# TensorE's order inside a step of the second attention: value and key products ahead of the output products

## What is computed

```python
q = (x @ w_q)...; k = (x @ w_k)...; v = (x @ w_v)...      # 32 query heads, 8 key/value heads of 128
lq = x @ w_lq; lk = (lq @ w_lk)...; lv = (x @ w_lv)...    # 32 latent key/value heads
q, k, lk = rope(q), rope(k), rope(lk)
attn = causal_attn(q, repeat(k, 4), repeat(v, 4), scale)
lat  = causal_attn(q, lk, lv, scale)
out = attn @ w_o + lat @ w_lo
```

## Time and profile before

| what | value |
|---|---|
| median of 3 runs | 2500.93 us (2497.93 to 2501.97) |
| the profiled execution | 2504.47 us, of it the span 2502.3 us |
| busy share of the span | PE 91%, PEld 80%, DVE 71%, ACT 58%, POOL 63% |
| mean granted TensorE clock | 0.955 of full |
| HBM over the span | 36 GB/s |

### The profile page before, as it was taken

How to read it: one execution, slowest core, us unless ns; L and a number is a source line. 1 busy time by engine, 2 the same in 40 slices (tenths; PEclk the granted TensorE clock), 3 DMA queues, 4 the chain that set the end, 5 groups by cost and what they waited for, 6 DMA issues and landing times. The chain is left out here.

```text
span 2502.3 us, 44127 instructions
## 1 busy us (share of the span) xinstructions
PE 2282.1 (91%) x14117; PEld 2003.4 (80%) x14117; DVE 1771.3 (71%) x3132; ACT 1452.4 (58%) x3980; POOL 1576.2 (63%) x1336
## 2 busy tenths in 40 slices
PE   7899999956999789999999999999999999987998
PEld 5888888843788688888888888888888888876886
DVE  5677677749522489888888888888888888972132
ACT  2667676630333267676666676676676776664332
POOL 3575757300344487887878878778878788751542
PEclk8999999975899899999999999999999999998999
DMA  3110101010000210111111101101111111003000
GB/s 99 33 42 23 44 22 51 1 43 0 1 1 1 73 50 25 55 38 43 47 39 48 52 19 54 56 25 55 39 38 52 39 45 43 18 5 144 1 17 17
DMA packets 41348, 93.68 MB, mean 37 GB/s; under 512 B 4836, under 2 KB 6760, under 8 KB 39808
## 3 DMA queue, kind: packets, MB, share of 16 engines
q1 hardware_dynamic: 41092, 90.55, 11.0%
HBM read 79.78 MB, written 10.75 MB: 36 GB/s over the span
## 5 line engine op out<-in xcount | busy, mean ns | idle before, releaser
L1138 POOL TENSOR_TENSOR a_nf_acc<-a_nf_acc,a_nf_term 128x512 f32<-128x512 f32 (+1 forms) x416 | 589.4, 1417 | 141.2 <-ACT a_nf_term L1232 74.1
L1618 POOL TENSOR_TENSOR f_w_lo<-WGU,f_w_hi 128x512 fp32r<-128x512 f32 x88 | 115.0, 1308 | 347.5 <-ACT f_w_hi L1634 347.3
L1192 ACT ACTIVATE a_probs<-bank,a_dip 128x128 f32<-128x128 f32 (+1 forms) x512 | 208.7, 420 | 194.3 <-DVE a_dip L1473 194.3
L1201 ACT ACTIVATE a_probs<-a_probs,a_share 128x128 f32<-128x128 f32 (+1 forms) x512 | 192.2, 461 | 68.8 <-DVE a_share L1479 68.8
L1119 POOL TENSOR_TENSOR a_qk_lo<-a_straight,a_qk_hi 128x512 fp32r<-128x512 f32 (+1 forms) x160 | 197.0, 1235 | 36.9 <-ACT a_qk_hi L1178 36.9
L1543 DVE TENSOR_SCALAR a_nf_term<-a_nf_unit 128x512 f32<-128x512 f32 (+1 forms) x288 | 211.8, 780 | 3.4 <-DVE a_nf_unit L1526 0.6
L63 PE MATMUL bank<-a_wo_hi,a_ot_hi 128*128 128x512 f32 x512 | 211.9, 414 | 0.0
L1484 DVE TENSOR_TENSOR a_pt_lo<-bank,a_pt_hi 128x384 fp32r<-128x384 f32 x256 | 140.8, 550 | 90.5 <-ACT a_pt_hi L1209 89.8
L65 PE MATMUL bank<-a_wo_hi,a_ot_lo 128*128 128x512 f32 x512 | 200.9, 392 | 0.0
L64 PE MATMUL bank<-a_wo_lo,a_ot_hi 128*128 128x512 f32 x512 | 200.5, 392 | 0.0
L1178 ACT ACTIVATE a_qk_hi<-a_straight 128x512 fp32r<-128x512 f32 (+1 forms) x160 | 94.3, 589 | 175.0 <-DVE a_straight L1458 175.0
(11 more groups left out here) (251 smaller groups left out, 8470.3 us busy)
## 6 DMA issues: line engine op xcount, KB each, us to landing
a_raw<-in_l_o SPq DMA_DIRECT2D x64, 256.0 KB, 2.6
a_raw<-in_l_vk SPq DMA_DIRECT2D x32, 384.0 KB, 3.1
a_raw<-in_l_ql SPq DMA_DIRECT2D x32, 320.0 KB, 2.9
a_raw<-in_l_ou SPq DMA_DIRECT2D x32, 288.0 KB, 2.8
n_codes<-coded_w SPq DMA_DIRECT2D x8, 1056.0 KB, 12.8
a_raw<-in_l_nr SPq DMA_DIRECT2D x16, 384.0 KB, 3.0
a_nf_raw<-in_w_nf SPq DMA_DIRECT2D x24, 256.0 KB, 2.6
coded_w<-a_nf_acc SPq DMA_DIRECT2D x24, 256.0 KB, 2.0
```

The costliest lines, as they stand in the source:

```text
L1138: pool.tensor_tensor(acc, left, nf_term[:, i % CODE_RING, 0:w], ALU.add).then_inc(nf_added, 1)
L1192: act.activation(probs[:, n % 2, col:col + keys], bank[:, at:at + keys], ACT.Exp, bias=dip[:, n % 2, i:i + 1], accum_out=total[:, n % 2, i ...
L1201: ins = act.activation(cell, cell, ACT.Copy, scale=share[:, n % 2, i:i + 1])
L1618: pool.tensor_tensor(lo, src, hi.bitcast(F32), ALU.subtract).then_inc(part_lo[i], 1)
```

## The change

In `l1_attention_block`'s TensorE program the loop over `units[1:]` moves from the end of a step to the place directly behind the first turn, ahead of `output` and of the second turn. No instruction is added or removed, and the programs of VectorE, ScalarE, GpSimd and SyncE are the same.

```diff
                     if not (first and n < 1):
                         turn(n - 1, 0)
+                    for name in units[1:]:
+                        project(name)
                     if not (first and n < 3):
                         output(n - 3)
                     if not (first and n < 1):
                         turn(n - 1, 1)
-                    for name in units[1:]:
-                        project(name)
```

## The result

The changed kernel takes 2744.15 us (median of 4 runs, 2740.32 to 2747.39) against 2501.45 us (2497.93 to 2506.54), a ratio of 1.0968 with a 95% interval of [1.0941, 1.0995]. The forecast was 2704 in 2630 to 2755. The sign and the range were right, and so was the mechanism of the stop; 40 us were missing from the sum, and one of its terms, a gain in (c), had the wrong sign. The profiled execution took 2741.0 us, and its span is 236.6 us longer than that of before.

What follows compares the result with a forecast made beforehand. The second attention was taken as bound by TensorE, busy 1286 of 1374 us. Terms 144 + 32 + 24 - 16 - 32 + 52 = +204 us on the profiled 2504.5 gave 2708, less 3.5 to the median: 2704 us, range 2630 to 2755.

Steps and rivals of the forecast that it cites:

- (c): VectorE's start and A unit read-out: later in steps 10 and 11, +24 us; earlier in steps 1, 5 and 9, -16.
- (a): Two-product steps: second product stays at its bank's read-out, output products and second turn fall behind it; 47 x 3.07, +144 us.
- 40 waits of the earlier trace: Sign, 16.0 us in 40 pieces: second products in nearly all 47 two-product steps already wait for L1455, the A unit's read-out.
- faster: Rival, two-product steps: A unit's read-out comes early enough, no stop, only gains of step 0 and (d) left; 2460 us, chance 0.04.
- (b): Steps 2, 6, 12 and 15: banks are freed later, so the A unit starts 0.9 us later, 1.5 in step 15; +32 us.
- The -16 us of (c): Steps 1, 5 and 9, behind a single product: VectorE's peaks start 0.8 us earlier, 0.4 in step 1; -16 us.
- (d): Second turn's wait for the first turn's low part goes in one-product steps, mainly 0 and 8; -32 us.
- (e): TensorE's clock falls to 0.50 behind 41 new stops, 1.5 us each, less six falls in step 0; +52 us.
- no fall of the clock: Rival: the clock does not fall behind the new stops; 2653 us, chance 0.17.
- shorter chain on VectorE: Rival: VectorE's coding terms shorten, giving back up to 1 us ahead of each read-out; 2658 us, chance 0.12.
- Longer stretches: Rival: second low-clock stretch in stops of 4 us and more, +80 for +52, up to 20 us delay; 2753 us, chance 0.15.

Runs made afterwards that it cites:

- experiment 2: Products moved only in the steps with two products, against the kernel before: 2743.66 us, ratio 1.0953.
- 3: Only each step's first product moved behind the first turn, a second product stays at the step's end, against the kernel before: 2507.59 us, ratio 1.0008.
- experiment 7: Changed kernel with VectorE's read-out of the A unit directly behind the peaks in steps with two products, against the kernel before: 2579.34 us, ratio 1.0304.
- the first pair of experiments: Products moved only in steps with one product (2500.46 us), or only in steps with two (2743.66 us), each against the kernel before.
- Experiment 1: Products moved only in the steps with one product, against the kernel before: 2500.46 us against 2506.27, ratio 0.9984.
- the second filler: Changed kernel with a pair's first product made once more, twice more in steps 5, 9 and 14, against the kernel before: 2676.93 us, ratio 1.0689.
- the early read-outs: A unit read out behind the peaks: changed kernel's pair steps 2579.34 us, kernel before's pair steps 2579.45, all steps of the changed kernel 2686.66.
- the first filler: Changed kernel with a pair's first product made once more, twice more in step 5, against the kernel before: 2699.23 us, ratio 1.0780.

## Why the prediction was right, and where it was short

**What holds the second product**, (a): right. The prediction read the 40 waits of the earlier trace rows as nearly all of the 47 second products, and that was too much. By the timeline 32 of them stand ahead of a second product, 0.28 us each, 30 in steps 5, 9, 11 and 14 and 2 in step 10; the other 8 are A units, 7 of them in step 15, 0.95 us each. Step 1 has no such wait, and its bank was free 0.15 to 1.6 us before the product came. So the waits were the sign in two thirds of the cases, and the distance from the read-out's end to the product's start would have been the better one. That the product could not move by 3 us, and that everything that stood ahead of it would then stand behind the stop, is shown by experiment 2 (pairs alone give the full loss), by 3 (with the second product back at the end there is none) and by 7 (with the release moved, the stop is gone). The rival *faster* named the point from which it would decide, a read-out that ends 3.3 us earlier; experiment 7 moves it by 3.9 us in steps 1 and 9 of group 3, and the stop goes.

**The late A units**, (b), and the part of (c) on steps 10 and 11: right in size, A units at 2.20 us in steps 2, 6, 10 and 12 and at 3.89 in step 15, as forecast. The peaks of steps 10 and 11 start at 3.72 and 3.27 us (3.74 and 3.6 forecast).

**The -16 us of (c)**: the step that failed. That "peaks can start at T + 2.16" in steps 1, 5 and 9 took for granted that VectorE had caught up by the start of the step, since the second turn and its high part come earlier. In the steps ahead, 0 and 8, I had shortened TensorE's time by (d), and not asked whether VectorE's time got shorter too. It did not. Steps 1 and 9, behind the steps that gained 2.30 and 1.82 us, started their second product 1.39 and 1.84 us later. Step 5 shows how far such a lag reaches. Step 4 ahead of it is as long as before, and yet in six of eight groups the second product of step 5 starts later. VectorE's peaks in group 1, counted from the scores, start at 3.72, 2.87, 2.49 and 2.91 us in steps 2 to 5, where before they started at 1.87, 1.89, 1.66 and 2.08: the lag left by step 1 is worked off slowly and is still 0.8 us in step 5. Either kernel of the first pair of experiments has it there too, and their peaks of step 5 start at 2.95 and 2.93 us, behind the shortened step 0 in the one and the stop of step 1 in the other. In group 3 they started at 3.22, 2.73, 2.48 and 2.92 already before the change, so nothing was left to lose there. So (c) was +41 in place of +8. Experiment 1 shows it without any pair moved, and it is the reason why the one-product moves gained 5 us and not 25. In steps 1 and 9 the prediction also took 0.8 us off both stops, though its own (c) gives step 1 only 0.4; and in (d), step 0 of group 6 waited 0.34 us and not 1.98 or more.

**The clock**, (e): the mechanism right, the size short. I had 41 falls less six of step 0, at 1.5 us each. The pairs have 42 and the six are gone, both nearly as forecast, though not step by step: the stops of steps 1 and 9 were 3.5 and 3.8 us and not 2.6, by (c) again, and all 16 brought a fall and not six in ten, while step 14 had its fall in only four of seven. What the forecast lacked are the seven falls in step 15, where the A unit waits 2.3 to 2.4 us, and three more. So there are 43 stretches more and not 35. Their price by the second filler is 1.6 us each, and 43 x 1.6 = 70 us is an estimate of the term from it; TensorE's busy time gives 80. I can't say which is nearer, since some of the slowed work may lie ahead of a stop and only shorten it.

**The sum against the two parts of the stage.** Idle time came to +155 against 152 forecast, clock to +80 against 52. The first agreement is in part luck: by the steps (c) was 33 us too small, the gains of (d) 8 too small and (b) 3 too large, so (a) to (d) add up to 174 and not 155. The step table and the division in idle and busy time cut the same 235 us in different ways (69 or 80 us for the clock), and the 19 us between 174 and 155 are not assigned. The 7 us by which the stage's 235 falls short of the 243 between the medians are for the most part the places of the two profiled executions beside their medians, 3.0 above and 3.2 below.

Of the rivals, *no fall of the clock* stands beside the second filler: 2653 was its price, and 2677 is measured with 11 of 52 stretches left. A *shorter chain on VectorE* did not come: the chain from the peaks to the end of the read-out takes 1582.47 - 1575.66 = 6.81 us in step 9, and took 1490.83 - 1484.00 = 6.83. In step 1 of four groups it is shorter, 6.82 instead of 7.30 us, half a microsecond where that rival wanted one in every pair. *Longer stretches* were nearer to the truth than the forecast, 9 us above the result, but in part for another reason: it had the delay pass on behind the stops, which happened in step 5 (some 5 us over all groups), while the larger delays, of steps 1 and 9, came from the short steps ahead of them. Its 80 us for the clock are what the busy time gives.

The page of the Trainium skill that speaks for this change (Perfetto Trace Analysis, "Optimizing Tensor Performance", Matmuls) says that independent groups of matmuls should rotate through PSUM banks, so that reading out one lies beside the next. This kernel rotates over two banks, in both orders. What the trace adds is that the rotation covers a read-out only if the matmuls between two uses of a bank last as long as VectorE takes to come to it: with the products pulled together the wait went from 16.0 to 200.2 us.

What stays open: the loss of the early read-outs was read from waits and starts and not taken apart by further runs, and whether a third ring bank would make the moved order pay was not tried.

## What to carry to other kernels

A product can be pulled ahead only as far as the release of its bank. Many short waits at its present place say that it is there already, if they are that product's: look at which instructions wait before counting them. Moving it ahead then moves only its cover behind the stop. Time saved on the bound engine in one step counts only if the second engine also has less to do before the next shared release; otherwise look at the next steps, since it is paid back there, here as many as four steps on. If a product waits for a bank, reorder the engine that frees it, by one instruction first: that was worth 1% here, where the reordering of the bound engine cost 10%.

## What was not expected of the hardware

Work without use made the kernel faster: repeated matmuls in the stops took 67 us off, since the granted clock of the stage went from 0.93 to 0.99. And the cost of slowed matmuls shows in this profile as *busy* time, up to 80 us more for the same instructions, so a busy share that stays high does not say that nothing was lost; the granted clock beside it does. The length of a pause did not decide by itself whether a fall came: none behind the 1.98 us of the earlier trace rows, falls behind rests of 2.04 and 1.98 us in steps 9 and 14 of the first filler. In the changed kernel the stop of 3.4 us in step 14 had no fall in three groups and one in four, and the wait of 2.3 to 2.4 us ahead of the A unit in step 15 had one in all seven that wait there. What decides between them these runs do not show.
